# Silu of the gate, second half of the step sizes and one late W tile moved by a few scans in a two-layer kernel (linear attention, then Mamba)

## What is computed

```python
mod = silu(c) @ W_ada + b_ada
shift, scale, gate = split(mod, 3)
h = layernorm(x, gamma, beta) * (1 + scale) + shift
h = h[:, perm]
xm, z = split(h @ W_in, 2)
xm = silu(conv4(xm) + conv_b)
dtr, Bm, Cm = split(xm @ W_xp, [64, 80])
dt = softplus(dtr @ W_dt + b_dt)
A = -exp(A_log)
# scan over the tokens
hst = hst * exp(dt_t * A) + (dt_t * x_t) * B_t
y_t = sum over the states of hst * C_t
y = (y + xm * D_param) * silu(z) @ W_out
out = x + gate * y[:, inv_perm]
```

## Time and profile before

| | us |
|---|---|
| median of 3 runs | 2984.08 |
| lowest, highest | 2979.17, 2987.91 |
| the profiled execution, its own time | 2985.57 |
| its span in the trace | 2983.8 |
| busy: TensorE | 2646.6 (89%) |
| busy: VectorE | 2453.0 (82%) |
| busy: ScalarE | 1624.0 (54%) |
| busy: GpSimd | 1880.5 (63%) |

### The profile page before, as it was taken

How to read it: one execution, slowest core, us unless ns; L and a number is a source line. 1 busy time by engine, 2 the same in 40 slices (tenths; PEclk the granted TensorE clock), 3 DMA queues, 4 the chain that set the end, 5 groups by cost and what they waited for, 6 DMA issues and landing times. The chain is left out here.

```text
span 2983.8 us, 31811 instructions
## 1 busy us (share of the span) xinstructions
PE 2646.6 (89%) x10790; PEld 1503.3 (50%) x10790; DVE 2453.0 (82%) x3111; ACT 1624.0 (54%) x2444; POOL 1880.5 (63%) x822
## 2 busy tenths in 40 slices
PE   7999999999999878988988988988998898897964
PEld 3555555555555344554554554454455455454542
DVE  3566566566566699999999999999999999999993
ACT  1231332332332566876875875776676677677550
POOL 0131122121132496897998899899799799889991
PEclk9999999999999878999999989999999998999976
DMA  6102131231234344555665675665575566566663
GB/s 217 36 29 92 64 113 36 92 113 64 92 112 130 107 103 95 122 115 129 150 149 127 142 165 111 148 154 125 141 161 126 133 154 138 131 146 141 164 126 72
DMA packets 261604, 355.39 MB, mean 119 GB/s; under 512 B 21597, under 2 KB 115937, under 8 KB 261434
## 3 DMA queue, kind: packets, MB, share of 16 engines
q1 hardware_dynamic: 202024, 246.38, 27.2%
q0 software_dynamic: 55680, 105.93, 20.4%
q10 hardware_dynamic: 3730, 0.96, 0.2%
HBM read 215.56 MB, written 71.58 MB: 96 GB/s over the span
## 5 line engine op out<-in xcount | busy, mean ns | idle before, releaser
L2077 POOL TENSOR_TENSOR hs<-slots,b_wide 128x2048 f32<-128x2048 f32 x255 | 1269.9, 5008 | 129.9 <-PE bank L1592 125.7
L2271 DVE TENSOR_TENSOR_SCAN hs<-bank,hs 128x512 f32<-128x512 f32 x1024 | 1226.6, 1218 | 27.1 <-ACT bank L1849 20.0
L1849 ACT ACTIVATE bank<-dt,decay 128x512 f32<-128x512 f32 x1022 | 699.7, 691 | 546.1 <-DVE hs L2271 541.6
L1592 PE MATMUL bank<-ident,hs 128*128 128x128 f32 x4096 | 672.8, 293 | 247.6 <-DVE acc L2289 215.3
L1592 PEld LDWEIGHTS bank<-ident,hs 128*128 128x128 f32 x4096 | 510.9, 150 | 732.2 <-DVE acc L2289 270.9
L2289 DVE SCALAR_TENSOR_TENSOR acc<-bank,c_t,acc 128x512 f32<-128x512 f32 x772 | 568.3, 736 | 34.6 <-PE bank L1592 29.4
L1544 PE MATMUL bank<-h_t,w_in 128*128 128x512 f32 x1024 | 505.7, 604 | 0.0
L2125 POOL DMA_DIRECT2D acc<-scaled x252 | 290.0, 1151 | 54.7 <-DMA acc<-scaled 36.8
L983 POOL TENSOR_TENSOR y_rs<-y_var,mhalf 128x8 f32<-128x8 f32 x8 | 15.8, 1971 | 389.1 <-DVE y_var L356 389.1
L1644 PE MATMUL bank<-w_y,values 128*128 128x512 f32 x512 | 256.8, 608 | 0.8 <-DVE values L2393 0.8
L1555 PE MATMUL bank<-w_out,h_in 128*128 128x512 f32 x448 | 225.3, 627 | 3.6 <-ACT dt L1816 3.5
(11 more groups left out here) (180 smaller groups left out, 3332.2 us busy)
## 6 DMA issues: line engine op xcount, KB each, us to landing
b_wide<-b_rows SPq DMA_DIRECT2D x256, 256.0 KB, 3.6
acc<-scaled POOLq DMA_DIRECT2D x252, 256.0 KB
w_in<-in_L_cond_W_in SPq DMA_DIRECT2D x128, 256.0 KB, 4.5
res<-in_x SPq DMA_DIRECT2D x8, 2048.0 KB, 10.0
h_tiles<-h_t SPq DMA_DIRECT2D x56, 256.0 KB, 2.7
h_in<-h_tiles SPq DMA_DIRECT2D x56, 256.0 KB, 5.0
x_rows<-w_part POOLq DMA_DIRECT2D x28, 512.0 KB, 6.7
x_rows<-res SPq DMA_DIRECT2D x6, 2048.0 KB, 7.3
```

Source lines behind the costliest of these rows:

```text
L1592: last = nc.tensor.transpose(bank[:, j * P:(j + 1) * P], hs[:, slot, j, t * P:(t + 1) * P], ident[:, :])
L1849: nc.scalar.activation(decay_banks[N % 3][:, :], dt[:, H % 2, j, :], ACT.Exp, scale=g.decay[:, 4 * (H % 2) + j, s:s + 1]).then_inc(da_read ...
L2077: nc.gpsimd.tensor_tensor(hs[:, U % RING, :, :], slots[:, H % SLOTS, :, :], b_wide[:, U % B_RING, :].unsqueeze(1).to_broadcast([P, 4, CHUNK]),
L2271: nc.vector.tensor_tensor_scan(block, decay_banks[N % 3][:, :], block, 0.0, ALU.mult, ALU.add).then_inc(scanned, 1)
```

## The change

Only tables of constants change. The Silu of the gate's second half goes from step 3 to step 8 of the next turn. The second half of the step sizes: dt products from 4, 5, 5, 6 to 6, 7, 7, 8; splits from 9, 10, 10, 11 to 11, 12, 12, 13; Exp from 12 to 14; Ln from 16 to 17. The first late W tile (tile 0 of a turn) is done at steps 3 and 4 in place of 7 and 8 and copied at step 8 in place of 13; in `batch_places` it thus takes its work bank before the four dt products in place of after them. What is computed stays the same.

```diff
-DT_AT = (85, 87, 91, 91, 4, 5, 5, 6)
+DT_AT = (85, 87, 91, 91, 6, 7, 7, 8)
...
-W_AT = (7, 11, 89, 101, 106, 110, 121, 130)
+W_AT = (3, 11, 89, 101, 106, 110, 121, 130)
...
-SILU_Z_AT = (104, 3)
+SILU_Z_AT = (104, 8)
...
-SPLIT_AT = (91, 92, 96, 96, 9, 10, 10, 11)
-EXP_AT = (97, 12)
-LOG_AT = (99, 16)
+SPLIT_AT = (91, 92, 96, 96, 11, 12, 12, 13)
+EXP_AT = (97, 14)
+LOG_AT = (99, 17)
...
-KEEP_W_AT = (13, 17, 95, 107, 112, 116, 127, 136)
+KEEP_W_AT = (8, 17, 95, 107, 112, 116, 127, 136)
```

## The result

| | before | after |
|---|---|---|
| median, us (20 runs each) | 2984.07 | 2989.24 |
| ratio, 95% interval | | 1.0019 [1.0013, 1.0025] |
| the profiled execution's span, us | 2983.8 | 2984.8 |

The change makes the kernel 5.2 us slower by the medians, 4 to 7.5 us by the interval. That is less than the 0.3% (9 us) that I called the bound, but with 20 runs each the interval excludes "no change". One of the runs before took 7310.65 us; it can't be part of a ratio of 1.0019, and the medians hardly feel it. The two profiled executions differ by only 1.0 us: before's took 1.5 us more than its kernel's median, after's (2986.67) 2.6 less. So the traces show where time moved, and the other 4.2 us have to be looked for in how executions differ.

What follows compares the result with a forecast made beforehand. VectorE's scans and additions set the pace, except where other engines hold its next stops. Turn 1's 1.6 + 0.3 us, other turns 0, sum to +1.9 on 2985.57: 2987.5, less 1.5 gives median 2986 us; range 2979 to 2993.

Steps and rivals of the forecast that it cites:

- my own signs of being wrong: Wrong if addition 9 waits under 2 us, any of turns 2-6 changes over 1 us, or scans 12-23 await decays.
- Scan 7's stall is hidden anyway: Turns 1 to 7: scan 7's 1.29 us decay wait goes (at most 9.0 us); addition 9 is late next.
- The late tile's 1.72 us: Turn heads: the moved tile's first matmul group delays the transposes for addition 9 by 1.72 us, at full clock.
- Turn 1 gets 1.9 us longer: Turn 1: 1.6 us from its head and 0.3 from the step sizes stay, as no GpSimd wait follows.
- Turns 2 to 6 stay as long: GpSimd's products at scans 28 and 48 absorb a later head; in turn 3 a TensorE bank wait does: 0 us.
- the chain of step sizes: Later splits, Exp and Ln, with waits for work banks, cost 0 to 0.5 us a turn; 0.3 taken in turn 1.
- the queues: SyncE's list and GpSimd's adding store stay in place; the moved tile's block still loads ahead of need: no cost.
- Turn 0 between -1 and +1: Turn 0, without a Silu: tile groups precede additions 9 and 10, dt products leave addition 11's 2.9 us wait; taken as 0.
- Turn 7 at 0: Turn 7, with no tile moved: ScalarE finishes decay 12 at about 2720.3, against scan 12's earlier start at 2720.26: 0 us.
- The slower rival: Low TensorE clock in the gap after turn heads: 9 us, 2993; decided once addition 17 waits over 1 us; chance 0.18.
- The faster rival: Turn heads: the moved tile costs nothing, clock back sooner or half clock covering less: 2979.5 us; chance 0.13.
- Dearer tables: A pause of a table load's length at the Silu's new place: turn 7 loses 2.6 us, 2988.5; chance 0.03.

Runs made afterwards that it cites:

- the light kernels: Two kernels with GpSimd's products of units 5 and 6 halved in turns 1 to 7: kernel before, 2976.31 us; changed kernel, 2986.55 us.
- the light kernel after: Changed kernel with GpSimd's products of units 5 and 6 made over half the columns in turns 1 to 7: 2986.55 us, ratio 1.0008.
- the filler: Three extra matmuls, never read, around the start of turns 1 to 7: on the changed kernel 2984.69 us, on the kernel before 2988.00 us.
- the Silu's experiment: Kernel before with only the gate's second Silu moved, from scan 3 to scan 8: 3000.89 us, ratio 1.0055.
- the power on ScalarE: Kernel before with the variance's power -1/2 taken off GpSimd and made by ScalarE as Ln and Exp: 2980.10 us, ratio 0.9981.

## Why the prediction was right, and where it wasn't

The forecast was 2986 us, the median 2989.24, inside 2979 to 2993 and within 0.3%. The number is in part luck, as the sum at the end shows, and two of my own signs of being wrong appeared: turns 3 and 4 changed by over 1 us, and decays were waited for at scan 21 of turn 0 (0.44 us) and scan 12 of turn 7 (0.50). By its own steps:

- **Scan 7's stall is hidden anyway**: right. It vanished in seven turns, and leaving the Silu out gains nothing that the runs can tell.
- **The late tile's 1.72 us**: right in turn 1 to a tenth. I had the transposes at 1271.63 - 1253.6 = 18.0 rel (measured 18.0), addition 10 at 20.9 (20.9), the statistics at 23.4 (23.3). In turn 2 they came at 22.8 rel, not at 23.8: there the clock had risen by the second group, and addition 9 waited 3.03 us, not 3.9. Over turns 1 to 6 it waited 3.0 to 4.1.
- **Turn 1 gets 1.9 us longer**: measured 1.8.
- **Turns 2 to 6 stay as long**: this step failed. They changed by -0.4, +1.9, +1.3, -0.6 and +0.9, in all +3.1. Turns 2 and 5, which had waits for GpSimd to give, did stay, and the light kernels show GpSimd's cover. Turn 3 has no such wait; its head became 1.7 us longer, not 0.8, and that it would fit "inside that" wait of 1.16 us was wrong: the wait was there again, 1.4 us. In turns 4 and 6 new waits stand behind the head.
- **"0 to 0.5 us a turn" for the chain of step sizes, and "no cost" for the queues**: the terms that were mis-sized. The second W tile begins at 33.1, 34.1, 34.2 and 34.3 rel in turns 2, 3, 4 and 6, where it began at 31.8, 32.1, 32.2 and 33.9. Addition 17 waits 0.9, 1.4, 2.6 and 1.5 us. I had its nearest row, the 1.16 us of the earlier trace rows, and gave it no weight. The splits are the smaller part of this. The transposes of y wait for one in turns 1, 3, 4 and 6, but that moves them only in turns 1 and 3, by 1.2 and 0.8 us from the turn's start; in turns 2, 4 and 6 they come when they came. The rest is low clock behind the gap in turns 2, 3 and 6 (in turn 2 the initial sums' eight matmuls take 1.90 us in place of 1.06) and, in turn 4, the block of h. The last can't be put down to the change: the light kernel after has the same head in turn 4 and no wait before addition 17. In turn 7 addition 14 waits 2.12 us for a dt product that stands 1.86 us behind a split and then runs at half clock.
- **Turn 0 between -1 and +1**: wrong, -3.0. The wait of 2.9 us before addition 11 went, as the text says it would, and I should have priced it.
- **Turn 7 at 0**: -0.7 us. Its scan 12 starts 0.50 us late for a decay, so ScalarE's slack was spent as worked out, and addition 14's wait was made up behind scan 28.
- **The slower rival**, low clock in the gap that follows, partly came true: addition 17 passed 1 us in turns 3, 4 and 6, and in turn 7 the low clock lay ahead of addition 14; in turn 2 it waited 0.9, in turns 1 and 5 not at all. Whether it also holds the missing 4.2 us of the median isn't shown: the 20 runs follow their clock, which speaks for it, but no slow execution's trace is at hand, and the filler that takes 4.5 of the 5.2 us away raises the clock at the head and not in that gap.
- **The faster rival** didn't occur. **Dearer tables**: no pause shows, the load takes 1.28 us and the function follows 1.29 to 1.30 us after the load's start in every turn, so the Trainium skill's drain (ScalarE: Activation LUTs, "What ACT_TABLE_LOAD costs") is again not borne out by this trace.

In the profiled execution the sum of -3.0, +1.8, +3.1, -0.7, +0.8 ahead of scan 0 and -1.0 behind the last scan is +1.0, near my +1.9, by two errors of opposite sign.

## What to carry to other kernels

When a long instruction is moved on an in-order engine, list what it will now stand in front of and which banks those copies and splits free; here moving one part without the others cost 10 to 17 us, and the visible stall was worth nothing. Take work from the engine that sets the next stop (4.2 us for moving one 1.7 us instruction a turn off GpSimd), not the wait that the timeline shows first. And judge a change of under 0.3% by many runs: here single profiled executions lay up to 9 us from their kernel's median.

## What the hardware did that I hadn't expected

- **Filling one gap of TensorE moves the low clock to the next.** With three more matmuls in the head of the kernel before, the granted clock there rose from 0.50 to 0.95, and the next idle time grew from 1.26 to 2.78 us, with half-clock transposes behind it. The same filler gave 4.5 us to one kernel and took 3.7 from another.
- **A gap's length alone didn't tell.** In turn 4 of the kernel after, 2.75 us of idle time left the clock up (0.63 us for the transposes of y); a group of W that had 1.89 us more ahead of it, 4.5 us on, ran at half clock. In the Silu's experiment 1.63 us were followed by half clock.
- **Executions of one kernel differ through the clock.** The kernel before with the filler took 2980.05 us in its profiled execution and 2988.0 in the median of 12 runs; scan 0, ahead of which nothing was changed, came anywhere from 1009.3 to 1015.2 us in the profiled executions.

**Left open and not tried**: loading the second W tile's block one unit earlier, which might take the 1.89 us of turn 4 away; work in the gap ahead of the transposes of y, together with the head's; and the power on ScalarE in the changed kernel.
